# A one-core transformer layer on Trainium2: GpSimd paced by half slots, and expert outputs gathered in single transfers

## The chip, the core and the metric

The kernel runs on one core of one Trainium2 chip. The metric is the time of one execution on the device in microseconds (us); lower is better. The core's engines run side by side, each with its own instruction stream: TensorE (PE; its weight loads are shown as PEld), VectorE (DVE), ScalarE (ACT), GpSimd (POOL) and SyncE (SP), which only issues DMAs. They wait for each other through semaphores.

## What is computed

Token rows are gathered from an embedding table (4 batches of 512 tokens, 256 columns, 16 heads of 16). Two blocks follow, each behind a layer norm and added to its input:

```
h = take(W, ids)                                        # (4, 512, 256)
h = h + local_attention(layernorm(h)) @ Wo + bo         # window 128, looks one window back, causal
z = layernorm(h)
h = h + full_attention(z)                               # no mask
      + sum over the 2 best of 8 experts of gate * (z @ W_expert + b_expert)
```

## The kernel before

**Stages and slots.** The attention runs in eight stages, `STAGES`: local 0, local 1, local 2, full 0, local 3, full 1, full 2, full 3 (numbers 0 to 7; the number behind the kind is the batch). A stage has 16 slots (`u`), each of two half slots (`t`, 0 to 31). In every slot PE computes transposed scores into `ST` (L1414 in full stages, L1420 in local ones), row scores into `SC` (L1392) and probabilities times values into `OB` (L1441). ACT turns `ST` into `prob` (L800), DVE reduces `SC` to row maxima (L933). `SC` has two banks, so PE can be at most two row scores ahead of DVE.

**The other work** (projections, output projection, gates, expert matmuls, sums) hangs on the half slots by the table `PREPS`: an entry `(what, batch, first)` in stage s means that its steps are counted from half slot `first` of that stage; a negative `first` continues an entry of the stage before. All five engines walk through the same table in program order. A place in the table is a place in an engine's queue, not a time: an engine that waits for nothing runs ahead of the others.

**The experts.** Batches 0 and 1 (q = 0), then 2 and 3 (q = 1), go through the experts together. GpSimd scatters the normalised rows into `x_sorted` (8 indirect DMAs for each batch, 16 for each q; L611, `sort_rows`, from step 4 of `route` on). 24 tiles of sorted rows then run through the experts, two in every second half slot: GpSimd gathers each tile's weights (L625, `gather_weights`, into a ring of six), SP loads the rows (L517), PE turns and multiplies them (L1310, L1325), DVE copies the result to `ys` (L1088), and SP stores it to `y_sorted` (L524). At last `combine`: GpSimd gathers each token's two expert outputs from `y_sorted` (L645, `gather_outputs`; per batch four tiles of tokens, two transfers each) into six buffers `y` that lie in `xT_local`, `xT_full` and `rest`, and DVE adds them to `h` with their weights (L1102, `add_outputs`, five steps after the gather). GpSimd also adds the full attention to `h` (L682, `add_attention`), which waits for DVE's L975, and does the masks of the local stages (L672) and a part of the projections (L658).

**Where GpSimd can run ahead.** Its loop over the half slots has no wait of its own. In a local stage the mask of a slot waits for that slot's probabilities; in a full stage only waits inside the jobs hold it back, so transfers of several half slots can be issued behind each other.

## Time and profile before

| | |
|---|---|
| median of 3 runs | 676.07 us (670.94 to 677.17) |
| the profiled execution | 671.74 us, with a span of 670.0 us from the first to the last instruction |
| PE busy | 550.9 us, 82% of the span |
| DVE busy | 418.2 us, 62% |
| ACT busy | 304.0 us, 45% |
| GpSimd busy | 236.5 us, 35% |
| mean granted TensorE clock | 0.919 of full speed |

Busy time of an indirect DMA on GpSimd is the time in which it makes the transfer's descriptors, not the time in which the data moves. A wait is listed with what ended it; "remote" means that a semaphore ended it and that the profile found no instruction that ended just then. "issue" means that the profile shows no wait that ended just then.

### The profile page before, as it was taken

Reading aid. Unit: us, or ns where it says so; the run is one execution under the profiler, and the core shown is the slowest. Engines: PE = TensorE matmul, PEld = TensorE weight load, DVE = VectorE, ACT = ScalarE, POOL = GpSimd, SP = SyncE. Lnnn points to the kernel's source line nnn. Section 1 sums busy time; section 2 is a strip of 40 time slices with the busy share of each in tenths; the row PEclk is TensorE's granted clock in tenths of the full one; section 3 lists DMA queues with packets and bytes.
Section 4 is the critical chain, followed back from the end, with each engine's and each line's share of the span. In section 5 each row is a group of like instructions: output and inputs, shape, how many; then the busy total and the mean of one; then the engine's idle time right before and its main releaser. Section 6 shows DMA issues by size and latency. Waiting matters only on the chain.

```text
span 670.0 us, 9773 instructions
## 1 busy us (share of the span) xinstructions
PE 550.9 (82%) x3352; PEld 280.3 (42%) x3352; DVE 418.2 (62%) x927; ACT 304.0 (45%) x570; POOL 236.5 (35%) x294
## 2 busy tenths in 40 slices
PE   4765998989999899998869899889948648999562
PEld 3443554755654344444424455443312224554110
DVE  7336756667687876676688557558836427757620
ACT  0312545536445655662433554346625414545452
POOL 3853235224223300215462324121164264430721
PEclk9968899899999999996967999999978788999957
DMA  6387515433532255233253486733263566851320
GB/s 166 110 174 154 115 49 159 80 64 96 112 81 83 91 144 126 77 99 95 76 170 109 152 210 200 188 96 94 72 165 95 141 188 174 275 166 49 87 71 32
DMA packets 48049, 81.81 MB, mean 122 GB/s; under 512 B 7672, under 2 KB 39040, under 8 KB 44928
## 3 DMA queue, kind: packets, MB, share of 16 engines
q1 hardware_dynamic: 40320, 58.11, 33.5%
q0 software_dynamic: 7680, 23.08, 11.7%
q8 instruction: 27, 0.44, 0.3%
q14 instruction: 22, 0.18, 0.1%
HBM read 52.59 MB, written 28.31 MB: 121 GB/s over the span
## 4 chain that ended last, share of the span: by engine, by line
PE 60%; DVE 20%; issue 10%; another core or an unknown queue 3%; ACT 2%; DMA 2%; POOL 1%; SPq 0%; POOLq 0%; DVEq 0%; ACTq 0%
PE OB L1441 11%; PE SC L1392 8%; PE R L1234 8%; DVE neg_max L933 6%; PE ST L1414 6%; PE R L1325 5%; PE R L1249 5%; PE SC L1397 3%; PE ST L1420 2%; DMA QS<-shiftT 2%; PE R L1310 2%; PE R L1282 2%; PE R L1340 2%; PE SC L1400 2%
## 5 line engine op out<-in xcount | busy, mean ns | idle before, releaser
L933 DVE TENSOR_REDUCE neg_max<-SC 128x1 f32<-128x512 f32 x256 | 169.5, 686 | 120.7 <-PE SC L1392 86.0
L800 ACT ACTIVATE prob<-ST 128x512 f32<-128x512 f32 x256 | 136.8, 600 | 106.4 <-PE ST L1414 84.3
L1392 PE MATMUL SC<-KS,QS 96*128 96x512 bf16 x256 | 99.4, 400 | 44.1 <-DVE neg_max L933 29.7
L1441 PE MATMUL OB<-prob,VS 128*32 128x512 f32 (+2 forms) x1024 | 113.4, 517 | 0.1
L803 ACT ACTIVATE prob<-ST 128x512 f32<-128x512 f32 (+1 forms) x128 | 68.6, 543 | 82.0 <-PE ST L1420 76.3
L1414 PE MATMUL ST<-QS,KS 98*128 98x512 bf16 x256 | 82.1, 396 | 13.8 <-issue 12.3
L672 POOL TENSOR_SCALAR_AFFINE_SELECT prob<-prob 128x512 f32<-128x512 f32 x64 | 41.0, 640 | 138.7 <-ACT prob L803 135.5
L1392 PEld LDWEIGHTS SC<-KS,QS 96*128 96x128 bf16 x256 | 25.2, 98 | 97.6 <-DVE neg_max L933 66.8
L941 DVE TENSOR_REDUCE neg_max<-SC 128x2 f32<-128x512 f32 x64 | 44.1, 688 | 24.8 <-PE SC L1400 24.4
L1397 PE MATMUL SC<-KS,QS 96*128 96x256 bf16 (+1 forms) x256 | 55.8, 271 | 2.9 <-DVE neg_max L938 1.7
L938 DVE TENSOR_REDUCE neg_max<-SC 128x1 f32<-128x128 f32 (+1 forms) x128 | 39.5, 350 | 28.0 <-PE SC L1400 26.6
L1420 PE MATMUL ST<-QS,KS 98*128 98x256 bf16 (+1 forms) x256 | 49.5, 277 | 7.8 <-DMA QS<-shiftT 7.8
L1400 PE MATMUL SC<-mask_q,ident_bf 128*128 128x128 bf16 x256 | 52.0, 227 | 0.0
L658 POOL TENSOR_TENSOR parts<-rest,parts 128x512 bf16<-128x512 f32 x32 | 37.3, 1168 | 38.8 <-ACT parts L745 38.7
L682 POOL TENSOR_TENSOR h<-h,AO 128x256 f32<-128x256 f32 x16 | 11.6, 728 | 107.0 <-DVE AO L975 94.5
L1414 PEld LDWEIGHTS ST<-QS,KS 98*128 98x128 bf16 x256 | 24.7, 99 | 50.7 <-issue 23.2
L740 ACT ACTIVATE parts<-R,qk_bias 128x512 bf16<-128x512 f32 x32 | 22.0, 687 | 50.9 <-PE R L1234 49.8
L906 DVE SCALAR_TENSOR_TENSOR rest<-R,qk_bias,parts 128x512 f32<-128x512 f32 x32 | 23.9, 747 | 26.4 <-ACT parts L740 22.9
L1234 PE MATMUL R<-xT_full,w_qkv 128*128 128x512 f32 x64 | 33.8, 610 | 4.6 <-DVE VS L918 2.6
L1397 PEld LDWEIGHTS SC<-KS,QS 96*128 96x128 bf16 x256 | 25.5, 102 | 25.7 <-issue 9.5
L1441 PEld LDWEIGHTS OB<-prob,VS 128*32 128x32 f32 x1024 | 20.7, 111 | 34.6 <-issue 27.6
L1420 PEld LDWEIGHTS ST<-QS,KS 98*128 98x128 bf16 x256 | 23.2, 104 | 24.4 <-issue 16.7
(139 smaller groups left out, 816.1 us busy)
## 6 DMA issues: line engine op xcount, KB each, us to landing
scratch<-parts SPq DMA_DIRECT2D x96, 128.0 KB
QS<-scratch SPq DMA_DIRECT2D x16, 384.0 KB, 5.4
KS<-scratch SPq DMA_DIRECT2D x16, 384.0 KB, 4.7
xs<-x_sorted SPq DMA_DIRECT2D x24, 256.0 KB
y_sorted<-ys SPq DMA_DIRECT2D x24, 256.0 KB
QS<-scratch SPq DMA_DIRECT2D x16, 256.0 KB, 3.9
KS<-scratch SPq DMA_DIRECT2D x16, 256.0 KB, 4.9
x_sorted<-ys SPq DMA_DIRECT2D x24, 128.0 KB, 3.6
```

What stands on the lines that cost most here:

```text
L672: pool.affine_select(out=own, in_=own, compare_op=ALU.is_ge, fill=0.0, base=0, pattern=[[0, GH], [1, P]], channel_multiplier=-1).then_inc( ...
L800: act.activation(prob[:, u % 2, e, :], src[:, :], ACT.Exp, scale=SCALE).then_inc(s_prob, 1)
L803: act.activation(prob_local[:, u % 2, u // 2 % 2, 2 * e:2 * e + 2, 0:w], src[:, :].rearrange("p (i w) -> p i w", i=2)[:, :, 0:w], ACT.Exp, ...
L933: dve.tensor_reduce(own_max[:, i, head:head + 1], bank[:, :], AX.X, ALU.max, negate=True).then_inc(s_max, 1)
L941: dve.tensor_reduce(own_max[:, 2:4, head], bank[:, :].rearrange("p (w k) -> p w k", w=2), AX.X, ALU.max, negate=True).then_inc(s_max, 1)
L1234: mm = pe.matmul(bank[:, :], w, xT_of(p)[:, c, :], start=(c == 0), stop=(c == NC - 1))
L1392: pe.matmul(bank[:, :], Q[0:SHIFT_ROW, head, i * P:(i + 1) * P], K[0:SHIFT_ROW, head, :], start=True, stop=True).then_inc(s_sc_ps, 1)
L1397: pe.matmul(bank[:, first:last], Q[0:SHIFT_ROW, head, w * P:(w + 1) * P], K[0:SHIFT_ROW, head, max(w - 1, 0) * P:(w + 1) * P], start=(w % ...
L1400: mm = pe.matmul(bank[:, last - P:last], ident_bf[:, :], mask_q[:, :], start=False, stop=(w % 2 == 1), skip_group_check=True)
L1414: mm = pe.matmul(bank[:, :], K[0:KROWS, g * GH + e, keys], Q[0:KROWS, g * GH + e, :], start=True, stop=True)
L1420: mm = pe.matmul(bank[:, i * 2 * P:i * 2 * P + w], K[0:KROWS, head, keys], Q[0:KROWS, head, kt * P:kt * P + w], start=(i == 0), stop=(i == 1),
L1441: mm = pe.matmul(OB[VW * i:VW * (i + 1), columns], VS[s % 3][:, kt, v:v + VW], p_of, start=(kt == 0), stop=(kt == NT - 1), skip_group_chec ...
```

## The change

1. `PREPS`: `combine` of batch 0 moves from half slot 18 of stage 6 to half slot 30 of stage 5; `combine` of batch 1 from half slot 22 to half slot 21 of stage 6. Batches 2 and 3 stay.
2. `GATHERS`: for batches 0 and 1 one transfer is issued in a half slot instead of two (8 half slots instead of 4), and DVE's adds stand in every second half slot instead of every one. Batches 2 and 3 stay at two transfers.
3. From stage 4 on GpSimd waits at every half slot until PE has computed that half slot's first transposed scores (`begun`, a wait on `s_st_ps`). 128 waits are added; no other instruction is added or removed.

```diff
--- before.py
+++ after.py
@@ -64,9 +64,9 @@
     2: (("full", 0, -23), ("out", 1, 0), ("local", 3, 9)),
     3: (("out", 2, 0), ("full", 1, 9)),
     4: (("full", 1, -23), ("route", 0, 1), ("full", 2, 1), ("experts", 0, 33)),
-    5: (("experts", 0, 1), ("out", 3, 0), ("full", 3, 9)),
-    6: (("full", 3, -23), ("route", 1, 1), ("experts", 1, 19), ("combine", 0, 18), ("combine", 1, 22)),
-    7: (("experts", 1, -13), ("combine", 2, 16), ("combine", 3, 20)),
+    5: (("experts", 0, 1), ("out", 3, 0), ("full", 3, 9), ("combine", 0, 30)),
+    6: (("full", 3, -23), ("combine", 0, -2), ("route", 1, 1), ("experts", 1, 19), ("combine", 1, 21)),
+    7: (("experts", 1, -13), ("combine", 1, -11), ("combine", 2, 16), ("combine", 3, 20)),
 }
 START_SLOTS = 36
 HALF_SLOTS = 2 * UNITS
@@ -86,6 +86,7 @@
 ROUTE_STEPS = 13
 SCATTER_STEP = 4
 SCATTERS = (1, 2)
+GATHERS = (1, 1, 2, 2)
 W_RING, X_RING, Y_RING = 6, 3, 3
 LOAD_STEP, W_STEP, STORE_STEP, ADD_STEP = -4, -3, 6, 5
 
@@ -133,6 +134,12 @@
     after = STAGES[s + 1][0]
     first, end = (-(-TILES[after] * LEAD[after] * (head - H + j) // LEAD[kind]) for j in (0, 1))
     return [(s + 1, k) for k in range(first, end)]
+
+
+def begun(s, t):
+
+    per = BANKS[STAGES[s][0]]
+    return SCORES_BEFORE[s] + per * (t // 2) + per // 2 * (t % 2) + 1
 
 
 def first_rows(t):
@@ -628,24 +635,23 @@
                     bass.IndirectOffsetOnAxis(ap=w_rows[:, j:j + 1].bitcast(U32), axis=0),
                 ).then_inc(s_w_exp[n % W_RING], 16)
 
-            def gather_outputs(b, t):
+            def gather_output(b, t, k):
                 q, n = b // 2, b * NT + t
-                if n == 0:
+                if n == 0 and k == 0:
                     p = STAGE[FULL, B - 1]
                     pool.wait_ge(s_wo_ps, at(B - 1, 2, 2))
                     pool.wait_ge(s_v_ps, V_BEFORE[p + 1])
                     pool.wait_ge(s_qk_ps, at(p, 4, 4))
                     pool.wait_ge(s_part2, at(p, 4, 4))
-                if b % 2 == 0 and t == 0:
-                    for k in range(Y_RING):
-                        pool.wait_ge(s_stored[k], ring_count((q + 1) * TILE_JOBS - Y_RING + k, Y_RING))
-                if n >= len(y):
+                if b % 2 == 0 and t == 0 and k == 0:
+                    for j in range(Y_RING):
+                        pool.wait_ge(s_stored[j], ring_count((q + 1) * TILE_JOBS - Y_RING + j, Y_RING))
+                if n >= len(y) and k == 0:
                     pool.wait_ge(s_moe, 2 * (n - len(y) + 1))
-                for k in range(TOP_K):
-                    pool.indirect_dma_start(
-                        y[n % len(y)][:, k, :], None, y_sorted[q],
-                        bass.IndirectOffsetOnAxis(ap=slots[q][:, b % 2 * NT + t, k:k + 1].bitcast(U32), axis=0),
-                    ).then_inc(s_y[n % len(y)], 16)
+                pool.indirect_dma_start(
+                    y[n % len(y)][:, k, :], None, y_sorted[q],
+                    bass.IndirectOffsetOnAxis(ap=slots[q][:, b % 2 * NT + t, k:k + 1].bitcast(U32), axis=0),
+                ).then_inc(s_y[n % len(y)], 16)
 
             def inv_std(p):
                 pool.wait_ge(s_mv, at(p, 2, 2))
@@ -699,8 +705,10 @@
                     for j in range(EXPERT_TILES):
                         if step == W_STEP + j:
                             gather_weights(b, j)
-                if what == "combine" and 0 <= step < NT:
-                    gather_outputs(b, step)
+                if what == "combine":
+                    for n in range(NT * TOP_K):
+                        if step == n // GATHERS[b]:
+                            gather_output(b, n // TOP_K, n % TOP_K)
 
             for t in range(START_SLOTS):
                 if t == 2:
@@ -721,6 +729,8 @@
                     if kind == LOCAL:
                         mask(s, u)
                     for t in (2 * u, 2 * u + 1):
+                        if s >= STAGE[LOCAL, B - 1]:
+                            pool.wait_ge(s_st_ps, begun(s, t))
                         for what, c, first in PREPS[s]:
                             prep(what, c, t - first)
                     group = output_turned(s, u)
@@ -1131,8 +1141,10 @@
                         row_slots(b)
                     if step == 3:
                         tile_experts(b)
-                if what == "combine" and ADD_STEP <= step < ADD_STEP + NT:
-                    add_outputs(b, step - ADD_STEP)
+                if what == "combine":
+                    for t in range(NT):
+                        if step == ADD_STEP + t * TOP_K // GATHERS[b]:
+                            add_outputs(b, t)
 
             def half_slot(s, t, rows):
 
```

GpSimd's queue at the end of stage 5 and the start of stage 6, before, with what each instruction waits for (`x_sorted<-xn` are scatters for the experts, `w_` the gathers of expert weights, `y_sorted` as source the gathers of outputs, `h<-h,AO` the adds of the attention):

```order
L682 TENSOR_TENSOR h<-h,AO 128x4x64 [waits biases_added,group_normalised] x2
L611 DMA x_sorted<-xn_local,slots 3072x256 [waits sorted_rows_turned,route_steps,sorted_rows_zeroed]
L611 DMA x_sorted<-xn_local,slots 3072x256 x7
L611 DMA x_sorted<-xn_full,slots 3072x256 x6
L682 TENSOR_TENSOR h<-h,AO 128x4x64 [waits biases_added,group_normalised]
L611 DMA x_sorted<-xn_full,slots 3072x256 x2
L625 DMA w_q<-in_L_ffn_W_experts,w_rows 128x512 [waits experts_in_psum,route_steps]
```

And now. `transposed_scores` is the new wait for the half slot:

```order
L688 TENSOR_TENSOR h<-h,AO 128x4x64 [waits biases_added,group_normalised]
L651 DMA xT_local<-y_sorted,slots 128x256 [waits qk_in_psum,part2,v_in_psum,ys_stored0,projected,ys_stored1,transposed_scores,ys_stored2]
L651 DMA xT_local<-y_sorted,slots 128x256 [waits transposed_scores] x3
L651 DMA xT_full<-y_sorted,slots 128x256 [waits transposed_scores] x2
L688 TENSOR_TENSOR h<-h,AO 128x4x64 [waits biases_added,group_normalised]
L651 DMA xT_full<-y_sorted,slots 128x256 [waits transposed_scores] x2
L618 DMA x_sorted<-xn_local,slots 3072x256 [waits sorted_rows_turned,route_steps,sorted_rows_zeroed]
L618 DMA x_sorted<-xn_local,slots 3072x256
L618 DMA x_sorted<-xn_local,slots 3072x256 [waits transposed_scores]
L618 DMA x_sorted<-xn_local,slots 3072x256
```

Eight output gathers of batch 0 have come in ahead of the 16 scatters, six of them between two adds of the attention, and the scatters are held in pairs by the new wait.

GpSimd's queue from the first expert weights of q = 1 on, before:

```order
L625 DMA w_q<-in_L_ffn_W_experts,w_rows 128x512 [waits experts_in_psum,route_steps]
L625 DMA w_k<-in_L_ffn_W_experts,w_rows 128x512 [waits experts_in_psum]
L625 DMA w_v<-in_L_ffn_W_experts,w_rows 128x512 [waits experts_in_psum]
L645 DMA xT_local<-y_sorted,slots 128x256 [waits ys_stored0,part2,ys_stored1,qk_in_psum,ys_stored2,v_in_psum,projected]
L645 DMA xT_local<-y_sorted,slots 128x256
L625 DMA w_exp<-in_L_ffn_W_experts,w_rows 128x512 [waits experts_in_psum]
L645 DMA xT_local<-y_sorted,slots 128x256 x2
L682 TENSOR_TENSOR h<-h,AO 128x4x64 [waits biases_added,group_normalised]
L625 DMA w_exp<-in_L_ffn_W_experts,w_rows 128x512 [waits experts_in_psum]
```

And now:

```order
L688 TENSOR_TENSOR h<-h,AO 128x4x64 [waits biases_added,group_normalised]
L632 DMA w_exp<-in_L_ffn_W_experts,w_rows 128x512 [waits experts_in_psum,transposed_scores] x2
L651 DMA rest<-y_sorted,slots 128x256
L632 DMA w_q<-in_L_ffn_W_experts,w_rows 128x512 [waits experts_in_psum,transposed_scores]
L651 DMA rest<-y_sorted,slots 128x256
L632 DMA w_k<-in_L_ffn_W_experts,w_rows 128x512 [waits experts_in_psum,transposed_scores]
L651 DMA rest<-y_sorted,slots 128x256
L632 DMA w_v<-in_L_ffn_W_experts,w_rows 128x512 [waits experts_in_psum,transposed_scores]
L651 DMA rest<-y_sorted,slots 128x256
L632 DMA w_exp<-in_L_ffn_W_experts,w_rows 128x512 [waits experts_in_psum,transposed_scores]
L651 DMA xT_local<-y_sorted,slots 128x256 [waits expert_output_added]
```

Where one weight gather and two output gathers of batches 0 and 1 stood for a half slot, there are now one weight gather and one output gather of batch 1, each half slot behind a wait.

DVE's queue in half slots 2 to 5 of stage 6, before:

```order
L1078 TENSOR_TENSOR h<-R,h 128x512
L933 TENSOR_REDUCE neg_max<-SC 128x1
L950 CAST shift<-neg_max 128x4x4
L952 TENSOR_TENSOR shift<-neg_max,shift 128x4x4
L1055 TENSOR_TENSOR picked<-pick,position 128x128
L1058 TENSOR_REDUCE slot_f<-picked 128x16
L1059 CAST slots<-slot_f 128x16
L933 TENSOR_REDUCE neg_max<-SC 128x1
```

And now, in the same place:

```order
L1088 TENSOR_TENSOR h<-R,h 128x512
L943 TENSOR_REDUCE neg_max<-SC 128x1
L960 CAST shift<-neg_max 128x4x4
L962 TENSOR_TENSOR shift<-neg_max,shift 128x4x4
L1112 SCALAR_TENSOR_TENSOR h<-xT_local,weight,h 128x256 x2
L1065 TENSOR_TENSOR picked<-pick,position 128x128
L1068 TENSOR_REDUCE slot_f<-picked 128x16
L1069 CAST slots<-slot_f 128x16
L943 TENSOR_REDUCE neg_max<-SC 128x1
```

The first two adds of batch 0 (one pair of instructions for each tile of tokens) stand in half slot 3, ahead of the last steps that give the scatters their row numbers; the other three pairs follow in half slots 5, 7 and 9.

## Rows read from the trace of the kernel before

**Rows 1.** Waits of DVE: in total, times, longest, in us

```profile
DVE neg_max L933 <- remote: 25.6, 4, 11.4
```

**Rows 2.** Timeline 480 to 504: start, duration, instruction, [idle before <- ended by]

```profile
483.49 1.15 POOL L611 DMA_INDIRECT x_sorted<-xn_local,slots  x1 [0.15 <-issue]
...
495.30 0.39 PE L1392 MATMUL SC<-KS,QS 96*128 96x512 bf16 x1 [1.17 <-issue]
...
500.08 0.96 POOL L611 DMA_INDIRECT x_sorted<-xn_full,slots  x1 [0.30 <-issue]
...
502.33 0.69 DVE L933 TENSOR_REDUCE neg_max<-SC 128x1 f32<-128x512 f32 x1 [7.09 <-remote]
...
503.08 0.61 PE L1392 MATMUL SC<-KS,QS 96*128 96x512 bf16 x1 [7.40 <-issue]
```

**Rows 3.** Timeline 505 to 545, the second run of transfers

```profile
511.13 0.98 POOL L611 DMA_INDIRECT x_sorted<-xn_full,slots  x1 [0.16 <-issue]
...
522.48 0.95 POOL L645 DMA_INDIRECT xT_local<-y_sorted,slots  x1 [0.30 <-issue]
...
526.35 0.61 PE L1392 MATMUL SC<-KS,QS 96*128 96x512 bf16 x1 [5.25 <-DVE neg_max L933]
```

**Rows 4.** Timeline 534 to 554, the third run

```profile
535.05 0.96 POOL L625 DMA_INDIRECT w_exp<-in_L_ffn_W_experts,w_rows  x1 [0.15 <-issue]
...
543.49 0.38 PE L1392 MATMUL SC<-KS,QS 96*128 96x512 bf16 x1
...
548.82 0.95 POOL L645 DMA_INDIRECT rest<-y_sorted,slots  x1 [0.30 <-issue]
...
553.09 0.61 PE L1392 MATMUL SC<-KS,QS 96*128 96x512 bf16 x1 [9.22 <-DVE neg_max L933]
```

**Rows 5.** Timeline 620 to 641, the fourth run, in stage 7

```profile
620.97 0.94 POOL L645 DMA_INDIRECT xT_full<-y_sorted,slots  x1 [22.37 <-DMA y_sorted<-ys]
...
628.83 0.82 PE L1414 MATMUL ST<-QS,KS 98*128 98x512 bf16 x3
...
632.50 0.95 POOL L645 DMA_INDIRECT xT_local<-y_sorted,slots  x1 [0.30 <-issue]
...
635.29 1.00 DVE L1102 SCALAR_TENSOR_TENSOR h<-xT_local,weight,h 128x256 f32<-128x256 f32 x2 [1.41 <-DMA xT_local<-y_sorted,slots]
...
640.00 0.61 PE L1414 MATMUL ST<-QS,KS 98*128 98x512 bf16 x1 [10.35 <-issue]
```

**Rows 6.** Timeline 366 to 377, the six first weight gathers

```profile
367.24 0.99 POOL L625 DMA_INDIRECT w_q<-in_L_ffn_W_experts,w_rows  x1 [0.46 <-issue]
...
373.55 0.95 POOL L625 DMA_INDIRECT w_exp<-in_L_ffn_W_experts,w_rows  x1 [0.30 <-issue]
...
375.81 1.29 DVE L933 TENSOR_REDUCE neg_max<-SC 128x1 f32<-128x512 f32 x2 [2.13 <-remote]
```

**Rows 7.** PE alone, 505 to 545: half slots 12, 17, 22, 24 of stage 6 begin

```profile
507.63 0.60 PE L1414 MATMUL ST<-QS,KS 98*128 98x512 bf16 x2
...
516.62 0.60 PE L1414 MATMUL ST<-QS,KS 98*128 98x512 bf16 x2
...
537.61 0.60 PE L1414 MATMUL ST<-QS,KS 98*128 98x512 bf16 x2
...
543.05 0.60 PE L1414 MATMUL ST<-QS,KS 98*128 98x512 bf16 x2
```

**Rows 8.** Busy time by window: us, PE, PEld, DVE, ACT, POOL busy, clock, DMA share, GB/s

```profile
468.00:483.50 15.50, 14.96 (x92) 5.56 (x92) 14.05 (x35) 9.73 (x18) 0.74 (x2) 1.00 0.21 69
503.00:511.00 8.00, 7.59 (x36) 2.06 (x36) 5.07 (x12) 4.34 (x8) 0.72 (x1) 0.75 0.12 34
```

**Rows 9.** SP's DMA issues: last stores of expert outputs, q = 0 and q = 1

```profile
473.09 0.46 SPq L524 DMA_DIRECT2D y_sorted<-ys  x1
...
617.31 0.95 SPq L524 DMA_DIRECT2D y_sorted<-ys  x2
```

**Rows 10.** DVE's timeline, 479 to 485: the row numbers of the scatters

```profile
480.36 0.28 DVE L1055 TENSOR_TENSOR picked<-pick,position 128x128 f32<-128x128 f32 x1
```

## The prediction, made before the changed kernel ran

> **What bounds the kernel now.** I read the waits first. DVE's row maxima wait four times, 25.6 us in all, for a semaphore whose update matches no instruction that ended just then [rows 1]. The timelines around these waits show the same picture each time. From 483.49 to 500.08 GpSimd starts 14 scatters, one each 1.28 us. PE's row score of 495.30 ends at 495.69; the reduction that needs only this score starts at 502.33, 6.6 us late, and PE's next matmul at 503.08, after 7.4 us of idle time [rows 2]. DVE, ACT and PE have nothing else to wait for. So what is late is the news of PE's finished work, and it comes 1.3 us after GpSimd's run ends (501.04 to 502.33). The second run lasts from 511.13 to 523.43, and PE idles 5.25 us up to 526.35 [rows 3]. The third, 12 transfers from 535.05 to 549.77, ends in 9.2 us of idle PE up to 553.09 [rows 4]. The fourth begins at 620.97 in stage 7: PE ends its scores at 629.65 and starts again at 640.00, 10.35 us later [rows 5]. Six weight gathers from 367.24 to 374.50 leave DVE idle for 2.13 us up to 375.81 [rows 6]. Five runs, five pauses: 34 us of 671.74, of which PE idles 32. A pause sets in 5 to 10 us after a run began. After a pause the matmuls run at the lower clock level, 1.2 GHz (0.61 us for one that took 0.39 before, [rows 2]); in the 8 us after the first pause the granted clock is 0.75 [rows 8], at most 2.0 us lost. I take 1.2 us for each of the first three.
>
> DVE's four waits of [rows 1] all lie in these runs. That GpSimd's unbroken run of transfers is the cause is a reading of five coincidences, not a measured fact. I build the sum on it, and the second rival on its failure. Elsewhere in stages 5 to 7 PE is busy nearly all the time, so work on GpSimd costs only through these pauses and through what it delivers late.
>
> **The change, part by part.** The waits themselves are cheap. In stage 4 each slot's mask already waits for that slot's probabilities, which PE's scores precede: nothing changes. In stage 5 the first six weight gathers are no longer one run: the third must wait for half slot 0 of stage 5, the next ones for 1, 2 and 3. That takes away the pause of [rows 6]: **-1.7 us** (0 if it stays). Later weight gathers wait for experts two half slots or less before their own half slot anyway; a delay up to one half slot is covered by the four to five half slots between gather and use.
>
> *Batch 0's gathers.* They are now first in line at half slot 30 of stage 5, but they need the last store of q = 0, which SP issues at 473.09, ending 473.55 [rows 9]. In stage 7 the last store's issue ended at 618.26 and the gather started at 620.97, 2.7 us later [rows 5, 9]; so the first starts at about 476.3, when PE has already reached half slot 2 of stage 6. The waits hold none of the first six: one each 1.26 us, until 483.8. The attention's add (0.7 us) and two more gathers follow, to 487.2. Then come the scatters, which began at 483.49 before. Behind the waiting gather on GpSimd only the add and these scatters are queued; SP's row loads need the scatters, but not before half slot 15.
>
> *DVE's adds.* A gather that starts at 632.50 has its add at 635.29, 2.8 us later [rows 5]. So the first tile of tokens is there at 476.3 + 1.3 + 2.8 = 480.4, and DVE comes to that place at 480.36 [rows 10]: a wait of 0 to 0.6 us. Each pair of adds takes 1.0 us [rows 5]. In this stretch DVE is busy 14.05 of 15.5 us [rows 8], so the pair of half slot 3 is paid in full, and of the three others in half slots 5, 7 and 9 I count half. Where they stood, beside the experts, PE's slots are longer (5.4 us for two half slots, [rows 7], against 3.6) with expert matmuls that DVE doesn't set, and I count nothing back. **+3.0 us** (0 to 4.6).
>
> The Trainium skill (DMA: Bandwidth & Descriptors, Anatomy of one DMA) fits a GpSimd transfer with 2.0 us plus bytes over 436 GB/s, 2.3 us for these 128 KB. By it the tile is there at 479.9 and the wait is surely nil; by the row it is 480.4, and the sum is the same within 0.6 us.
>
> *The first pause.* The run now begins at 476.3 instead of 483.49. Let the pause set in at 484, PE being in half slot 5 or 6. Here the new wait acts: with PE's news late, GpSimd sees no further half slot begin and may issue only what is released, the last gathers and the pair of scatters of half slot 5, until 489.7. The pause ends 1.3 to 2.5 us later, near 491.5: 7.5 us, as long as the 7.4 of before. **0.** The other scatters are two to a half slot, 2.5 us of issue in half slots that take 1.8 us each (507.63 to 516.62 for five, [rows 7]), so GpSimd falls behind again and runs without a gap for 8 to 12 transfers: I add **+2 us** for a second, short pause (0 to 8).
>
> *The second pause.* The 10 transfers of [rows 3] were 2 scatters, 4 weight gathers and 4 output gathers. The output gathers are gone, and the weights come one to a half slot, 1.26 us of issue in 1.8. I take the pause away: 5.25 + 1.2 = **-6.5 us** (-6.5 to -3).
>
> *The third pause.* The 12 transfers of [rows 4] were three for each half slot. Now there are two, from half slot 21 to 28, 5.0 us of issue in a slot of 5.4 (537.61 to 543.05, [rows 7]). The gaps are 0.4 us, where 0.3 us lies between transfers anyway, so I don't expect it to vanish. But again GpSimd can issue only what has begun, at most four transfers. I take two pauses of 2 to 2.5 us for one of 9.2 with its 1.2 of slow clock: **-6 us** (-12 to 0).
>
> *The fourth pause* stays: batches 2 and 3 keep two transfers a half slot, and the gathers start only when the last store has landed, at 620.97 [rows 5], when half slots 16 and 17 of stage 7 have already begun. **0** (-6 to +2).
>
> Sum: -1.7 + 3.0 + 0 + 2 - 6.5 - 6 = -9.2 us, against the profiled execution's 671.74: 662.5. The median of the three runs, 676.07, stands 4.3 us above this execution; I allow 1.5 us for that and say **664 us**, 1.8% below the median.
>
> **The rivals.** *First, all of stage 6's pauses go.* A wait at each half slot could already be gap enough; then the first pause's 7.4 + 1.2, the second's 6.5 and the third's 10.4 go, with 1.7 of stage 5, and 3 for the adds stays: 671.7 - 24.2 = 647.5. For it: no pause stands in stage 4, where pairs of scatters alternate with masks. Against it: the runs of stage 6 keep next to no gap by the arithmetic above.
>
> *Second, the pauses move and don't shrink,* because their cause is not the unbroken issue but, say, the number of transfers in flight, or other DMA traffic: 671.7 + 3 for the adds, less some luck, 668 to 677, no measurable change. For it: the pauses set in after 5 us in one run and 10 in another, which a plain count of transfers doesn't give. Against it: all five coincide with runs, and none lies elsewhere.
>
> The Trainium skill (SBUF — State Buffer, Who interferes with whom) speaks for this rival: its rule is that "PE and ACT never wait on anyone", and GpSimd's interference is with VectorE alone. By that rule spacing the transfers frees nothing on PE, and the time is the second rival's; by rows 2 to 6 PE's idle time follows GpSimd's runs. No run yet separates the two.
>
> *Third, slower.* 8 gathers and 14 scatters stand in one line from 476.3 on, 28 us of issue with only one add of 0.7 us between. If the new waits hold GpSimd less than I think, because PE's scores of the next half slots are told before the freeze, the pause lasts from 484 to 505.5 instead of 7.4 us: +14; with the third pause unchanged the sum is 671.7 - 1.7 + 3 + 14 - 6.5 = 680.5. It decides from about 12 us of first pause on. Against it: in [rows 2] PE starts one more score after 494 and then nothing, so half slots that have begun can't pile up during a pause.
>
> **How the numbers follow.** Chances: my forecast 0.40, the first rival 0.18, the second 0.28, the third 0.14. The forecast's own range is 654 to 672, from the bounds of the second, third and adds' terms. The whole range, to hold 8 in 10, reaches to both outer cases: 646 to 680. A measurement of this kernel can tell about 1% from no change. Faster by over 1% (below 669.3) holds nearly all of the forecast and the first rival, 0.56; within 1%, the second and the forecast's upper end, 0.31; slower, the third, 0.13.
>
> **What would show it.** In the new profile: the first output gather near 476 to 477, the scatters from about 487; no idle time of PE over 3 us between half slots 14 and 19 of stage 6; shorter ones between 21 and 28; one of about 10 us near the end of stage 7; and DVE's waits for a "remote" semaphore down from 25.6 us to under 15. The prediction is wrong if pauses of the old length stand beside short runs of transfers, or if GpSimd's waits for its half slots show up as late weights at the expert matmuls.

## The result and the profile after

The changed kernel takes 650.26 us (median of 4 runs, 646.69 to 653.42) against 673.51 us (4 runs, 669.59 to 677.17) of the kernel before: a ratio of 0.9641, 95% interval 0.9599 to 0.9683, 3.6% faster. The forecast was 664 us, 1.8% faster: the direction and the range hold, the gain is twice as large. On other chips it is different, and that is the larger surprise; the experiments come to it.

The profiled execution took 652.53 us, its span is 650.8 us against 670.0 us before, at a mean granted clock of 0.933 against 0.919. The lines of after bear other numbers: L943 is L933 of before, L1404 is L1392, L1426 is L1414, L1453 is L1441, L1112 is L1102, L651 is L645, L618 is L611, L632 is L625, L810 is L800.

The three largest waits of the kernel after for a semaphore whose update matches no instruction that ended just then (in total, times, longest, in us):

```profile
ACT prob L810 <- remote: 9.9, 4, 4.5
DVE neg_max L943 <- remote: 7.4, 3, 3.6
ACT shiftT L790 <- remote: 7.3, 1, 7.3
```

DVE's 25.6 us of [rows 1] have become 7.4. To see where the time went, I cut stages 6 and 7 at the same half slots in both kernels, by the starts of PE's first transposed scores of half slots 0, 12, 19 and 30 of stage 6 and 22 of stage 7. The windows of before (in each: length, PE busy and instructions, the other engines, granted clock, DMA):

```profile
core 0: us, PE busy (x) PEld busy (x) DVE busy (x) ACT busy (x) POOL busy (x), PEclk, DMA share, GB/s
471.30:507.60 36.30, 25.26 (x126) 7.64 (x125) 21.07 (x44) 15.33 (x28) 14.33 (x15) 0.81 0.41 114
507.60:526.70 19.10, 10.95 (x57) 2.95 (x56) 9.83 (x18) 8.34 (x16) 10.28 (x11) 0.93 0.60 163
526.70:573.20 46.50, 35.19 (x173) 17.55 (x172) 24.73 (x49) 17.30 (x32) 22.29 (x24) 0.85 0.54 147
573.20:628.80 55.60, 53.60 (x293) 25.24 (x291) 37.75 (x70) 31.50 (x59) 16.34 (x18) 1.00 0.48 156
628.80:670.00 41.20, 17.03 (x78) 3.70 (x76) 8.38 (x19) 12.17 (x23) 12.23 (x14) 0.68 0.20 61
```

and the same of after:

```profile
471.60:510.00 38.40, 28.93 (x127) 8.16 (x126) 25.14 (x52) 15.33 (x28) 22.24 (x23) 0.78 0.49 132
510.00:521.20 11.20, 10.47 (x58) 2.95 (x57) 9.52 (x18) 8.40 (x16) 5.07 (x6) 1.00 0.32 105
521.20:556.80 35.60, 32.59 (x174) 17.19 (x173) 20.93 (x40) 17.22 (x32) 19.17 (x22) 0.95 0.82 219
556.80:613.00 56.20, 53.54 (x293) 25.21 (x291) 38.01 (x70) 30.73 (x58) 17.24 (x19) 1.00 0.48 156
613.00:650.80 37.80, 15.59 (x78) 3.62 (x76) 8.28 (x19) 12.92 (x25) 12.25 (x14) 0.75 0.22 66
```

PE issues the same matmuls. The second window loses 7.9 us: PE's idle time falls from 8.15 to 0.73. The third loses 10.9: 8.3 us of idle time, and 2.6 of busy time because the clock is granted at 0.95 instead of 0.85. The last loses 3.4, the first gains 2.1, the fourth 0.6.

The first window of after in the timeline (start, duration, instruction, [idle before <- ended by]):

```profile
478.52 0.96 POOL L651 DMA_INDIRECT xT_local<-y_sorted,slots  x1 [11.12 <-DMA y_sorted<-ys]
...
482.69 1.01 DVE L1112 SCALAR_TENSOR_TENSOR h<-xT_local,weight,h 128x256 f32<-128x256 f32 x2 [1.75 <-DMA xT_local<-y_sorted,slots]
...
485.30 0.61 PE L1404 MATMUL SC<-KS,QS 96*128 96x512 bf16 x1 [3.25 <-issue]
...
489.48 1.01 POOL L618 DMA_INDIRECT x_sorted<-xn_local,slots  x1 [0.30 <-issue]
...
493.82 0.61 PE L1404 MATMUL SC<-KS,QS 96*128 96x512 bf16 x1
...
497.23 0.69 DVE L943 TENSOR_REDUCE neg_max<-SC 128x1 f32<-128x512 f32 x1 [3.59 <-remote]
497.51 0.97 POOL L618 DMA_INDIRECT x_sorted<-xn_local,slots  x1 [0.53 <-remote]
...
497.98 0.39 PE L1404 MATMUL SC<-KS,QS 96*128 96x512 bf16 x1 [2.31 <-issue]
...
501.26 0.97 POOL L618 DMA_INDIRECT x_sorted<-xn_full,slots  x1 [1.51 <-remote]
```

The first output gather starts 2.2 us later than forecast, the scatters at 489.48. The pause of [rows 2], 7.40 us in one piece, is gone. What is late now are the maxima of 497.23: DVE waits 3.59 us for them, 2.8 of these after PE's score of 493.82 had ended (494.43), and PE idles 2.31 us up to 497.98; GpSimd's own waits for its half slots (497.51 and 501.26) stand beside it. The 3.25 us up to 485.30 are not of this kind: the adds of batch 0 stand ahead of the maxima in DVE's queue, and the first pair waits 1.75 us for its tile (482.69). In the window PE's idle time falls from 11.0 to 9.5 us, and its busy time grows by 3.7, at a clock of 0.78. The end of stage 7:

```profile
605.00 0.94 POOL L651 DMA_INDIRECT xT_full<-y_sorted,slots  x1 [21.89 <-PE ST L1426]
...
619.20 0.94 POOL L651 DMA_INDIRECT xT_local<-y_sorted,slots  x1 [0.30 <-issue]
622.28 0.57 ACT L790 COPY shiftT<-R 8x512 bf16<-8x512 bf16 x1 [7.32 <-remote]
622.55 0.94 POOL L651 DMA_INDIRECT xT_full<-y_sorted,slots  x1 [2.41 <-remote]
623.39 0.61 PE L1426 MATMUL ST<-QS,KS 98*128 98x512 bf16 x1 [7.99 <-ACT prob L810]
```

Here GpSimd issues 12 transfers in a row from 605.00, then has to wait for half slot 22. PE's news reaches ACT at 622.28, 2.1 us after GpSimd fell still (619.20 + 0.94), and PE's idle time is 7.99 us instead of the 10.35 of [rows 5].

### The profile page after: what moved, and what is told of

The parts are those of the page before. It is cut to its first block, busy times and chain, and to the rows that moved or that the text cites. A ratio compares the mean times of both kernels' runs of the same rounds, so it can differ in the third digit from the quotient of the medians.

```text
span 650.8 us, 9845 instructions
## 1 busy us (share of the span) xinstructions
PE 547.8 (84%) x3352; PEld 279.3 (43%) x3352; DVE 416.7 (64%) x927; ACT 304.0 (47%) x570; POOL 237.5 (36%) x294
## 3 DMA queue, kind: packets, MB, share of 16 engines
q0 software_dynamic: 7680, 23.08, 11.7%
## 4 chain that ended last, share of the span: by engine, by line
PE 63%; DVE 20%; issue 7%; DMA 2%; POOL 2%; ACT 2%; another core or an unknown queue 2%; SPq 0%; POOLq 0%; DVEq 0%; ACTq 0%
PE OB L1453 12%; PE SC L1404 8%; PE R L1246 8%; PE R L1337 7%; DVE neg_max L943 6%; PE ST L1426 6%; PE R L1261 5%; PE SC L1409 3%; PE R L1322 3%; PE ST L1432 3%; DMA QS<-shiftT 2%; PE R L1294 2%; PE R L1352 2%; PE SC L1412 2%
## 5 line engine op out<-in xcount | busy, mean ns | idle before, releaser
L943 DVE TENSOR_REDUCE neg_max<-SC 128x1 f32<-128x512 f32 x256 | 169.0, 685 | 102.4 <-PE SC L1404 85.5
L810 ACT ACTIVATE prob<-ST 128x512 f32<-128x512 f32 x256 | 137.1, 600 | 101.5 <-PE ST L1426 80.7
L1404 PE MATMUL SC<-KS,QS 96*128 96x512 bf16 x256 | 98.8, 398 | 29.8 <-DVE neg_max L943 16.7
L1453 PE MATMUL OB<-prob,VS 128*32 128x512 f32 (+2 forms) x1024 | 113.5, 517 | 0.1
L1426 PE MATMUL ST<-QS,KS 98*128 98x512 bf16 x256 | 80.9, 391 | 11.3 <-ACT prob L810 9.1
L1404 PEld LDWEIGHTS SC<-KS,QS 96*128 96x128 bf16 x256 | 25.1, 98 | 84.7 <-DVE neg_max L943 51.8
L951 DVE TENSOR_REDUCE neg_max<-SC 128x2 f32<-128x512 f32 x64 | 44.0, 688 | 25.6 <-PE SC L1412 25.3
L664 POOL TENSOR_TENSOR parts<-rest,parts 128x512 bf16<-128x512 f32 x32 | 37.7, 1181 | 37.4 <-ACT parts L755 26.5
L750 ACT ACTIVATE parts<-R,qk_bias 128x512 bf16<-128x512 f32 x32 | 22.0, 687 | 50.3 <-PE R L1246 48.7
L1426 PEld LDWEIGHTS ST<-QS,KS 98*128 98x128 bf16 x256 | 24.8, 99 | 47.0 <-ACT prob L810 22.3
L1409 PEld LDWEIGHTS SC<-KS,QS 96*128 96x128 bf16 x256 | 25.6, 102 | 26.5 <-issue 9.3
L688 POOL TENSOR_TENSOR h<-h,AO 128x256 f32<-128x256 f32 x16 | 11.6, 727 | 64.8 <-DVE AO L985 56.4
L1453 PEld LDWEIGHTS OB<-prob,VS 128*32 128x32 f32 x1024 | 20.7, 111 | 33.2 <-issue 28.2
```

The source lines that it names most:

```text
L810: act.activation(prob[:, u % 2, e, :], src[:, :], ACT.Exp, scale=SCALE).then_inc(s_prob, 1)
L943: dve.tensor_reduce(own_max[:, i, head:head + 1], bank[:, :], AX.X, ALU.max, negate=True).then_inc(s_max, 1)
L951: dve.tensor_reduce(own_max[:, 2:4, head], bank[:, :].rearrange("p (w k) -> p w k", w=2), AX.X, ALU.max, negate=True).then_inc(s_max, 1)
L1404: pe.matmul(bank[:, :], Q[0:SHIFT_ROW, head, i * P:(i + 1) * P], K[0:SHIFT_ROW, head, :], start=True, stop=True).then_inc(s_sc_ps, 1)
L1409: pe.matmul(bank[:, first:last], Q[0:SHIFT_ROW, head, w * P:(w + 1) * P], K[0:SHIFT_ROW, head, max(w - 1, 0) * P:(w + 1) * P], start=(w % ...
L1426: mm = pe.matmul(bank[:, :], K[0:KROWS, g * GH + e, keys], Q[0:KROWS, g * GH + e, :], start=True, stop=True)
```

## The experiments

**Theory A**: while GpSimd issues indirect transfers without a break, the semaphore updates of PE (news of finished matmuls) reach the other engines late, after 5 to 10 us of such a run, and are let through when GpSimd pauses. The new waits are a feedback: once PE's news is late, GpSimd runs out of released work and stops. **Theory B**: the pauses come from the number of transfers or the traffic, and waits alone change nothing; the gain is that of the moved gathers.

*The parts of the change.* `waits_only` and `waits_2` are one kernel: the kernel before with the waits alone.

```diff
                     for t in (2 * u, 2 * u + 1):
+                        if s >= STAGE[LOCAL, B - 1]:
+                            pool.wait_ge(s_st_ps, begun(s, t))
                         for what, c, first in PREPS[s]:
```

> The kernel before with the third part of the change alone: from stage 4 on GpSimd waits for every half slot; the table and the gathers stay two to a half slot. Theory A (PE's news is late once GpSimd has issued indirect DMAs without a break for 5 to 10 us, and a wait that stops GpSimd ends the lateness): the waits cut the runs of 14, 10, 12 and 16 transfers as soon as PE stands still, so the pauses of 7.4, 5.3, 9.2 and 10.4 us shrink by a third to a half each; time 655 to 663. Theory B (the pauses come from the number or the traffic of the transfers, the gain of the change from moving the gathers out of the expert part): no pause shrinks by more than 1 us; 668 to 675.

> The waits alone, again. Theory A: on a chip with pauses in the kernel before, they cut the runs of transfers and shorten the pauses of 7.4, 5.3, 9.2 and 10.4 us by a third to a half: ratio 0.975 to 0.99. On a chip without pauses 1.00. Theory B (the gain comes from the moved gathers): 1.00 on both.

`moves_only` and `moves_2` are the changed kernel without these two lines.

> The changed kernel without its waits: the gathers of batches 0 and 1 moved and one to a half slot in the table, but nothing holds GpSimd. Theory A: 8 gathers and 14 scatters follow each other with one add of 0.7 us between, from about 478 on; PE pauses from about 486 to 507, some 15 to 20 us instead of 7.4; the second pause is gone (-6.5), the third is a run of 12 to 16 and stays near 9; 670 to 682. Theory B: the waits do nothing, and the time is that of the changed kernel, 647 to 654.

> The moved gathers without the waits, again. Theory A: on a chip with pauses, the unbroken run of 22 transfers from 478 on makes one of 15 to 20 us; ratio 0.99 to 1.02. On a chip without, 1.009 as before. Theory B: 0.965 on a chip with pauses.

`after_2` and `after_3` are the changed kernel itself.

> The changed kernel again, beside the kernel before. On the chip of the four runs so far PE's news was never late and the kernel before took 624.9 us; on the chip of the prediction's runs it took 673.5. Theory A (lateness of PE's news during GpSimd's runs is a property of some chips, and the change gains only there): where the kernel before takes 670 or more, the change gives 0.96 to 0.97; where it takes about 625, it gives 1.00 to 1.01, since the moved adds cost and no pause is there to save. Theory B (the change gains by its order of work too): under 0.99 on either chip.

> The changed kernel again, as the partner of the two kernels with breaks. On a chip with pauses (kernel before about 674 us) 648 to 653 us, ratio 0.96 to 0.972. On a chip without (about 625 us) only the moved adds and gathers show: ratio 1.000 to 1.010, 625 to 631 us; if the new waits of GpSimd cost something by themselves it would be above 1.010.

Two kinds of chip came up in these runs. On chips 9 and 7 the kernel before takes 625 us (19 runs each), on chips 3, 2 and 1 it takes 674:

| kernel | chip 3 (before 673.99) | chip 9 or 7 (before 624.86, 625.00) |
|---|---|---|
| waits alone | 658.70, 0.9772 (0.9699 to 0.9844) | 625.13, 1.0006 (0.9981 to 1.0030) |
| moves alone | 664.36, 0.9855 (0.9791 to 0.9920) | 630.59, 1.0090 (1.0064 to 1.0115) |
| both | 650.99, 0.9679 (0.9596 to 0.9762) | 630.78, 1.0090 (1.0062 to 1.0119) |

On chip 3 the first two rows rest on two runs each and the third on three. The chip of the result, which is not named, behaves as chip 3. On chips 9 and 7 the change makes the kernel 0.9% slower, all of it by the moves, and the waits cost nothing. There is no pause there: in none of the traces from them does any engine wait for a "remote" semaphore, though GpSimd issues as densely (the kernel before itself has no trace from such a chip; its nearest are `run12` and the waits alone). The last run of the changed kernel on chip 7 (start, duration, instruction, [idle before <- ended by]):

```profile
593.61 0.95 POOL L651 DMA_INDIRECT xT_full<-y_sorted,slots  x1 [21.88 <-PE ST L1426]
...
604.22 0.82 PE L1426 MATMUL ST<-QS,KS 98*128 98x512 bf16 x3 [0.54 <-DMA QS<-shiftT]
...
605.36 0.39 PE L1426 MATMUL ST<-QS,KS 98*128 98x512 bf16 x1 [0.32 <-ACT prob L810]
...
612.68 0.95 POOL L651 DMA_INDIRECT xT_full<-y_sorted,slots  x1 [0.30 <-issue]
```

Sixteen transfers stand without a gap from 593.61 to 613.63, and PE waits 0.3 to 0.5 us between its scores, not 8 to 10.

On chip 3 both parts gain (2.3% and 1.5%), and together 3.2%, which the intervals don't tell from the sum. Neither theory says all of that. Theory B falls with `waits_2`, and its 0.965 for `moves_2` is missed as well. A is borne out by the ratio of `waits_2`, though not pause by pause, and missed by `moves_2`: I had expected 0.99 to 1.02 and a pause of 15 to 20 us. In lengths between half slots, in us (worked out from the traces as above; the kernel before on the result's chip, `late_moves` and `mid_moves` of further below on chips 2 and 1, waits alone on chip 9 as the one without pauses):

| | stage 6, 0 to 12 | 12 to 19 | 19 to 24 | 24 to stage 7 | stage 7, 0 to 22 | 22 to 31 | 31 to end |
|---|---|---|---|---|---|---|---|
| before | 36.3 | 19.1 | 16.4 | 35.6 | 50.1 | 25.5 | 15.7 |
| waits_2 | 31.2 | 14.4 | 21.1 | 33.7 | 50.3 | 21.3 | 15.7 |
| moves_2 | 44.6 | 14.7 | 15.4 | 26.5 | 50.3 | 26.6 | 15.7 |
| after_2 | 38.9 | 11.2 | 14.9 | 27.3 | 50.4 | 22.0 | 15.7 |
| late_moves | 32.8 | 11.4 | 18.4 | 27.6 | 58.1 | 21.7 | 15.7 |
| mid_moves | 32.3 | 17.9 | 17.4 | 27.5 | 50.3 | 22.2 | 15.7 |
| waits_only, chip 9 | 26.1 | 11.7 | 14.9 | 24.5 | 49.8 | 11.6 | 16.1 |
| after_3, chip 7 | 29.7 | 11.1 | 18.9 | 22.8 | 49.8 | 11.5 | 16.4 |

The waits alone shorten the first pause (half slots 0 to 12, by 5.1 us) and the one at the end of stage 7 (by 4.2). The second they only move on: half slots 12 to 24 take 35.5 us with them and without, and the third shrinks by 1.9. The moves alone thin out what lies behind half slot 12, at the price of 8.3 us ahead of it, where 8 gathers and 14 scatters now stand in one run with one add between. Two late waits beside that run in `moves_2`, of DVE and ACT, one of its later scatters, and ACT's wait at the end of stage 7:

```profile
496.44 0.69 DVE L941 TENSOR_REDUCE neg_max<-SC 128x1 f32<-128x512 f32 x1 [5.68 <-remote]
497.92 0.60 ACT L808 ACTIVATE prob<-ST 128x512 f32<-128x512 f32 x1 [8.69 <-remote]
...
502.49 0.97 POOL L618 DMA_INDIRECT x_sorted<-xn_full,slots  x1 [0.30 <-issue]
...
633.86 0.57 ACT L788 COPY shiftT<-R 8x512 bf16<-8x512 bf16 x1 [12.93 <-remote]
```

The last row is the end of stage 7 without the new waits: ACT waits 12.9 us behind the unbroken 16 transfers, against 7.32 us in the changed kernel. The first two show something that Theory A hadn't said: PE's news came through at 496.44 and 497.92 although GpSimd went on issuing until 503.46. In the kernel before the fourth pause ends in the same way:

```profile
637.91 0.57 ACT L780 COPY shiftT<-R 8x512 bf16<-8x512 bf16 x1 [9.18 <-remote]
...
640.01 0.95 POOL L645 DMA_INDIRECT xT_full<-y_sorted,slots  x1 [0.30 <-issue]
```

So the end of a run isn't what every pause waits for; late news also arrives in the middle of a run, and what lets it through then stays open. That explains why `moves_2` has two pauses of PE (5.73 us up to 497.19 and 3.85 up to 503.03) and not one of 15 to 20.

The price of the moves without pauses is read from chips 9 and 7: `after_3` against `waits_only` is 3.6 us longer in half slots 0 to 12 and 4.0 in 19 to 24, and 1.7 shorter behind. How it is shared out is less sure than the sum: `moves_only` against `run12` (30.8, 11.2, 17.0 and 22.8 us in stage 6 against 26.0, 11.2, 16.0 and 24.0) makes it 4.8, 1.0 and −1.2, with 4.6 us in all against 5.3. At the first of these places in `moves_only`:

```profile
480.36 1.00 DVE L1110 SCALAR_TENSOR_TENSOR h<-xT_local,weight,h 128x256 f32<-128x256 f32 x2 [1.28 <-DMA xT_local<-y_sorted,slots]
...
483.01 0.61 PE L1402 MATMUL SC<-KS,QS 96*128 96x512 bf16 x1 [2.62 <-DVE neg_max L941]
```

DVE waits 1.28 us for the first tile of tokens, adds it in 1.00, and PE idles 2.62 us for the maxima queued behind.

*A pause made on purpose.* `run12` and `run12_2` are the kernel before with 12 extra gathers of 128 KB in one run in stage 3, where no pause was; they land in buffers that are free then, and nothing uses what they bring.

```diff
+            def extra_run():
+                pool.wait_ge(s_st_ps, begun(3, 16))
+                for k in range(12):
+                    dst = (w_exp[3 + k // 2] if k < 6 else xs[(k - 6) // 2])[:, k % 2, :]
+                    pool.indirect_dma_start(dst, None, tok_w,
+                        bass.IndirectOffsetOnAxis(ap=ids[:, k:k + 1].bitcast(U32), axis=0),
+                    ).then_inc(s_extra, 16)
```

Left out of this cut and of the next two are the new semaphore and the waits of GpSimd and SP for all 12 landings, which stand ahead of the first expert weights and the first expert rows.

> The kernel before with 12 more indirect gathers of 128 rows of the embedding table (128 KB each) into buffers that are free then, issued by GpSimd behind each other at half slot 16 of stage 3, where no pause stood. Nothing uses what they fetch; GpSimd and SP wait for them only in stage 4. Theory A: 12 transfers take 15 us of issue; PE's news is late from 6 to 10 us after the first on and comes 1 to 2.5 us after the last: a new pause of 6 to 10 us in stage 3, span 676 to 681. Theory B (other traffic or places make the pauses): no idle time of PE over 3 us there, span within 2 us of 670.

> Twelve additional gathers in one run in stage 3, again. Theory A: on a chip with pauses a new one of 6 to 10 us in stage 3, PE idle from about 265 to 273; on a chip without, none. Theory B (the pauses need something else of stages 6 and 7): none in stage 3 on either.

`run12_gap4`, `run12_gap4_2` and `run12_gap4_3` have the same 12 with two breaks:

```diff
+                    if k in (3, 7):
+                        pool.wait_ge(s_extra, 16 * (k + 1))
```

> The same 12 additional gathers at the same place, but after the 4th and the 8th GpSimd waits until they have landed (about 1.8 us). Theory A: runs of four are too short for a pause, or a break of 1.8 us ends the lateness: idle time of PE there under 2 us, span 670 to 673. Theory B: what counts is the number or the bytes, so this does what the run of 12 does, whatever that is.

> The kernel before with the same 12 extra row gathers in the first full stage as in the run of 12, but now GpSimd waits after the 4th and the 8th until all issued so far have landed, a break of 1.5 to 2 us each time. Theory A (TensorE's news is held back while GpSimd issues indirect transfers without a break, and is let through once it pauses for 1.2 us or more): no new pause or one under 2 us at 259 to 280 us, time 671 to 675 against 673 to 674 of the kernel before on such a chip. Rival (the number of transfers counts, by the bytes or descriptors they put into the queues): a pause of 5 us or more as in the unbroken run, 678 to 682. On a chip where the kernel before takes about 625 us neither shows.

> The same kernel as the one with 12 extra gathers and breaks after the 4th and 8th, whose first two runs fell on a chip that has no pauses. Theory A (TensorE's news is held back while GpSimd issues indirect transfers without a break, let through once it pauses): on a chip with pauses no new pause or one under 2 us at 259 to 280 us, time 671 to 675 where the kernel before takes 673 to 674. Rival (the number of transfers counts): a pause of 5 us or more, 678 to 682. Where the kernel before takes about 625 us neither shows.

`run12_sp` issues 12 plain transfers of the same size into the same buffers from SP's queue instead:

```diff
+                        for k in range(12):
+                            dst = (w_exp[3 + k // 2] if k < 6 else xs[(k - 6) // 2])[:, k % 2, :]
+                            sp.dma_start(dst, tok_w[k * P:(k + 1) * P, :]).then_inc(s_extra, 16)
```

> The kernel before, with 12 plain transfers of 128 KB each issued by the SP queue in the place where the run of 12 GpSimd gathers stood (first full stage), into the same buffers. Theory A (GpSimd's issuing of indirect transfers is what holds TensorE's news back): no new pause at 258 to 275 us, the half slots 19 to 21 of that stage about 4 us apart, 672 to 675 where the kernel before takes 674. Rival (any 1.5 MB of traffic does): half slots 7 us apart as with the 12 gathers, 678 to 682. On a chip without pauses it tells nothing.

On chips 9 and 7 none of them shows anything (623.98, 626.26, and 625.43 us at 1.0002, 0.9971 to 1.0033). On the others:

| kernel | chip | half slots 19, 20, 21 of stage 3 start at | time, ratio |
|---|---|---|---|
| before | of the result | 266.6, 270.0, 274.0 | |
| 12 in one run (`run12_2`) | 3 | 267.5, 275.2, 282.0 | 680.77 (one run; before 673.99) |
| 4 + 4 + 4 (`run12_gap4_3`) | 2 | 266.0, 269.4, 273.4 | 675.35, 1.0001 (0.9960 to 1.0041) |
| 12 plain ones from SP (`run12_sp`) | 1 | 267.2, 270.5, 274.5 | 675.28, 1.0015 (0.9993 to 1.0037) |

The unbroken run, `run12_2`:

```profile
258.76 1.08 POOL L719 DMA_INDIRECT w_exp<-in_L_tok_W,ids  x1 [5.67 <-PE ST L1435]
...
267.98 0.38 PE L1413 MATMUL SC<-KS,QS 96*128 96x512 bf16 x1
...
272.45 0.69 DVE L954 TENSOR_REDUCE neg_max<-SC 128x1 f32<-128x512 f32 x1 [3.88 <-remote]
272.66 0.94 POOL L719 DMA_INDIRECT xs<-in_L_tok_W,ids  x1 [0.30 <-issue]
273.85 1.12 PE L1361 MATMUL R<-ident,OT 128*128 128x128 f32 x4 [3.41 <-DVE rest L927]
```

and with breaks, `run12_gap4_3`:

```profile
266.62 0.95 POOL L719 DMA_INDIRECT w_exp<-in_L_tok_W,ids  x1 [4.54 <-DMA w_exp<-in_L_tok_W,ids]
266.86 0.69 DVE L956 TENSOR_REDUCE neg_max<-SC 128x1 f32<-128x512 f32 x1 [0.42 <-PE SC L1415]
...
273.58 0.95 POOL L719 DMA_INDIRECT xs<-in_L_tok_W,ids  x1 [2.26 <-DMA xs<-in_L_tok_W,ids]
```

In the first the score of 267.98 ends at 268.36 and its reduction starts at 272.45; the news that is late is 9.6 us younger than the first transfer. From the start of half slot 19 to that of 21 it takes 14.5 us where it took 7.4. Up to the start of half slot 22, a stretch with the same matmuls, it is 17.7 us against 9.7, at a granted clock of 0.71 against 1.00: 3.7 us more of idle time and 4.3 more of busy time, so the slow clock costs more than the standing still. In the second the same reduction waits 0.42 us.

So 12 transfers in one run make a pause, 12 in three runs don't, and the same 1.5 MB from SP's queue doesn't. The number of the transfers isn't the cause; the unbroken issuing on GpSimd is, and this half of Theory A stands for this kind of chip. The other half, that the news is let through when GpSimd pauses, fails here too: the reduction of 272.45 starts before the 12th transfer (272.66). Three things limit the result. The unbroken run is a single execution. The three kernels ran on three chips, so a difference between those chips isn't excluded. And SP issues its 12 in 5.8 us, GpSimd in 14.8: that traffic kept up as long as GpSimd's, or plain transfers from GpSimd, would do nothing is not tested.

*Where the gathers stand.* `late_moves` keeps the waits and one output gather a half slot, but begins at half slot 18 of stage 6 as before (batch 1 behind batch 0), with the stores of the results to match (left out of the cut):

```diff
-    5: (("experts", 0, 1), ("out", 3, 0), ("full", 3, 9), ("combine", 0, 30)),
-    6: (("full", 3, -23), ("combine", 0, -2), ("route", 1, 1), ("experts", 1, 19), ("combine", 1, 21)),
-    7: (("experts", 1, -13), ("combine", 1, -11), ("combine", 2, 16), ("combine", 3, 20)),
+    5: (("experts", 0, 1), ("out", 3, 0), ("full", 3, 9)),
+    6: (("full", 3, -23), ("route", 1, 1), ("experts", 1, 19), ("combine", 0, 18), ("combine", 1, 26)),
+    7: (("experts", 1, -13), ("combine", 1, -6), ("combine", 2, 16), ("combine", 3, 20)),
```

> The changed kernel with batch 0's and batch 1's output gathers still one transfer a half slot and with the new waits, but begun where they stood before (half slot 18 of the second-last stage), batch 1's behind them to half slot 33; the adds and the stores of these batches later to match. Theory A (the feedback and the spreading bring the gain, the earlier place costs the adds on VectorE 0.9% on a chip without pauses): 0.96 to 0.97 of the kernel before where it takes about 674 us, and 0.997 to 1.003 where it takes about 625 us. Rival C (the earlier place is what brings the moves' gain, since it thins the half slots 16 to 32 of the second-last stage): 0.975 to 0.985, as the waits alone, on a chip with pauses; and on one without them 1.005 or more, since the late adds stand where TensorE runs at its upper clock.

657.28 us on chip 2, 0.9764 (0.9693 to 0.9836): in all no more than the waits alone. But stage 6 is 10.2 us shorter than with these (90.2 us for 100.4, in the table above), and even 2.1 shorter than in `after_2`. What that gains is lost behind: the first 22 half slots of stage 7 take 58.1 us instead of 50.3, because output gathers now stand up to its half slot 1, beside the weight gathers, and a pause falls there:

```profile
562.77 0.69 DVE L943 TENSOR_REDUCE neg_max<-SC 128x1 f32<-128x512 f32 x1 [5.56 <-remote]
```

`mid_moves` puts batch 0 at half slot 13, behind the scatters, and leaves batch 1 at 21.

> The changed kernel, with batch 0's output gathers begun at half slot 13 of the second-last stage, behind the first half slots' scatters (5 to 12) instead of ahead of them, one a half slot to 20; batch 1's stay at 21. The adds follow (half slots 18, 20, 22, 24). Theory A (the 8 gathers from 478 us and the 8 first scatters behind them are one unbroken run, and its adds block VectorE at half slots 3 to 9): where the kernel before takes about 674 us the pauses at 490 to 502 us become shorter, and 0.955 to 0.968; where it takes about 625 us the changed kernel's loss of 0.9% goes, 0.998 to 1.004. Rival D (half slots 13 to 20 then hold 16 weight gathers and output gathers, a new unbroken run, as where the gathers stood in their old place): 0.970 to 0.980 on a chip with pauses, and 1.000 to 1.006 on one without.

656.23 us on chip 1, 0.9724 (0.9694 to 0.9754). The stretch of half slots 0 to 12 takes 32.3 us instead of the 38.9 of the changed kernel, and 12 to 24 takes 35.3 instead of 26.1. The scatters end, and the gathers go on in their stead:

```profile
515.51 1.30 ACT L810 ACTIVATE prob<-ST 128x512 f32<-128x512 f32 x2 [2.97 <-remote]
515.75 0.95 POOL L632 DMA_INDIRECT w_k<-in_L_ffn_W_experts,w_rows  x1 [1.25 <-remote]
...
541.07 0.59 ACT L783 COPY xsT<-R 128x512 f32<-128x512 f32 x1 [3.78 <-remote]
541.94 0.95 POOL L632 DMA_INDIRECT w_v<-in_L_ffn_W_experts,w_rows  x1 [2.73 <-remote]
```

So the early place is what the moves' gain comes from: it keeps the stretch of the expert weights free of output gathers. Spreading them in the late place thins that stretch as well, but only pushes the pause into stage 7. The three kernels ran on different chips. The intervals of `late_moves` and `mid_moves` lie just clear of the changed kernel's first one (0.9599 to 0.9683), and meet that of `after_2` (0.9596 to 0.9762).

*Breaks for the changed kernel.* `after_gap4` lets GpSimd wait for the landing after every 4th scatter and every 4th output gather of batches 2 and 3, `after_gap2` after every 2nd, `last_gap` and `last_gap_2`, which are one kernel, only after every 4th of the last 16 gathers (this is their edit; the other two have the like behind the scatters too):

```diff
                 ).then_inc(s_y[n % len(y)], 16)
+                if b >= 2 and (t * TOP_K + k + 1) % 4 == 0:
+                    pool.wait_ge(s_y[n % len(y)], 2 * ring_count(n, len(y)))
```

> The changed kernel, with GpSimd waiting for the landing after every 4th scatter of the rows and after every 4th output gather of batches 2 and 3 (about 1.8 us each, 12 breaks). Theory A: what is left of the pauses, at the first scatters (3 to 4 us of idle TensorE), at the second ones (about 3) and at 620 us (8), goes to a large part: 10 us or more below the changed kernel, 636 to 643 us where that takes 650, pauses of TensorE each under 2.5 us. Rival B (GpSimd's breaks make its own work late: the scatters end 6 us later and the expert loads with them): no gain or a loss, 650 to 656. On a chip without pauses: within 0.3% of the changed kernel by A, 0.5% or more slower by B.

> As the one with a break after every 4th transfer, but after every 2nd (24 breaks, 43 us of waiting in all). Theory A with a limit between 2 and 4 transfers in a row: 3 us or more below the version with breaks after 4. If 4 in a row are already harmless: equal to it within 2 us, or slower by what the longer scatter run makes late (the second pair's scatters then take about 40 us instead of 20 and the expert loads behind them start late): up to 5 us slower.

These two ran on chip 7: 647.11 us, 1.0328 (1.0277 to 1.0379), and 672.02 us, 1.0751 (1.0706 to 1.0795), where the changed kernel has 1.009. Theory A's "within 0.3%" for `after_gap4` on such a chip is missed, and the rival holds: where there is no pause to remove, breaks only make GpSimd late. In `after_gap4` the scatters of q = 1 end late, and PE waits for their rows:

```profile
527.34 1.10 PE L1327 MATMUL R<-ident,xs 128*128 128x128 f32 x4 [7.18 <-DMA xs<-x_sorted]
```

15.57 us stand in that place with breaks after every 2nd. Neither was run on a chip with pauses.

> The changed kernel, with GpSimd waiting for the landing after every 4th of the last 16 output gathers (batches 2 and 3), nothing else. Theory A: on a chip with pauses the one at 612 to 620 us (8 us of idle TensorE) shrinks to under 3 us, but each break makes the last adds later (2 to 5 us from the end by the run with breaks everywhere): together 645 to 650 us, ratio 0.957 to 0.966. Rival (what is left at 620 us has another cause): the pause stays and the breaks cost 4 to 6 us, 654 to 657, ratio 0.971 to 0.977. On a chip without pauses: 4 to 6 us slower than the changed kernel, 1.015 to 1.019.

> The same kernel as last_gap (the changed one with breaks after every 4th of the last 16 output gathers), in more rounds. Theory A: on a chip with pauses 0.955 to 0.962 of the kernel before, below the changed kernel's 0.964 and 0.968. If its first result was luck: 0.963 to 0.970. On a chip without pauses the breaks only make the last adds later: 1.015 to 1.019 against the changed kernel's 1.009; above 1.009 by 0.005 at least.

On chip 1 `last_gap` takes 646.98 us, 0.9585 (0.9522 to 0.9648), the lowest ratio of this study, though its interval meets those of the changed kernel. Half slots 22 to 31 of stage 7 take 12.6 us instead of 22.0, the length of a chip without pauses; half slot 31 to the end takes 20.1 instead of 15.7, because the last adds wait for the last gathers:

```profile
611.34 0.94 POOL L651 DMA_INDIRECT rest<-y_sorted,slots  x1 [2.07 <-DMA xT_full<-y_sorted,slots]
...
625.05 1.14 POOL L651 DMA_INDIRECT xT_full<-y_sorted,slots  x1 [2.03 <-DMA xT_local<-y_sorted,slots]
...
629.28 1.00 DVE L1114 SCALAR_TENSOR_TENSOR h<-xT_full,weight,h 128x256 f32<-128x256 f32 x2 [3.40 <-DMA xT_full<-y_sorted,slots]
```

A gain of 9.4 us for a loss of 4.4. On chip 10 (before 626.61) only the losses remain, that of the moves and that of the breaks: 638.00 us, 1.0172 (1.0119 to 1.0225), with 21.5 us from half slot 31 to the end against the 16.4 of `after_3`. The remaining pause at the end was of the same cause. No version here is best on both kinds of chip: the waits alone cost nothing on the one and gain 2.3% on the other.

## Why the prediction was right and where it was wrong

The gain was forecast at 9.2 us and measured at 19.2. The cause was right; the step that failed is the sizing of the pauses, of the third one first (−6 for −10.9), then of the fourth (0 for −3.4), the stretch of the first (+5 for +2.1) and the second (−6.5 for −7.9). A later start of stage 4 (2.0) and 0.6 us in stage 7 go the other way.

*What bounds the kernel*: right on these chips. "What is late is the news of PE's finished work" holds, and GpSimd's unbroken runs are the cause (`run12_2` against `run12_gap4_3` and `run12_sp`, with the limits said there). Not right is that the news waits for the end of the run: that fits four of the five pauses of [rows 2 to 6], but the fourth is over while GpSimd still issues (637.91 and 640.01 above). The first pause also sets in later than the "5 to 10 us" of the prediction: PE's idle time begins at 495.69, 12.2 us after the first transfer. The second rival falls for these chips. The Trainium skill's rule that spoke for it (SBUF — State Buffer, Who interferes with whom: "PE and ACT never wait on anyone") doesn't help it: in `run12_2` PE idles 3.41 us up to 273.85 beside a GpSimd that only issues transfers, by way of late news, while the page speaks of the memory's ports. On chips 9, 7 and 10 PE has no such wait.

*The pause of stage 5*, −1.7 us: of that size between the two profiles (stage 4 begins 2.0 us later in after, stage 6 only 0.3 later), but not shown as I argued it. Four weight gathers still go in one run, and DVE's wait of 2.13 us [rows 6] has a like one in after:

```profile
371.92 0.95 POOL L632 DMA_INDIRECT w_exp<-in_L_ffn_W_experts,w_rows  x1 [0.30 <-issue]
374.19 0.94 POOL L632 DMA_INDIRECT w_exp<-in_L_ffn_W_experts,w_rows  x1 [1.33 <-PE ST L1426]
```

```profile
373.93 1.29 DVE L943 TENSOR_REDUCE neg_max<-SC 128x1 f32<-128x512 f32 x2 [2.07 <-PE SC L1404]
```

Stage 5 takes 102.2 to 102.6 us in every kernel with the waits on such chips (`waits_2`, `after_2`, `late_moves`, `mid_moves`, `last_gap`) and 103.2 to 103.3 in before, `moves_2` and `run12_2`, but 105.4 and 105.5 in `run12_gap4_3` and `run12_sp`, which lack the waits as well. By these traces the waits take at least 0.6 us off stage 5; how much more, and by which wait, is open.

*The adds*, +3.0 us: near for their first place (3.6 to 4.8 us on chips without pauses), but I counted nothing where gathers and adds of batch 1 stand; there half slots 19 to 24 grow by 1.0 to 4.0 us and the rest of the stage shrinks by 1.2 to 1.7. The moves cost 4.6 to 5.3 us in all without pauses, not 3.0. The first gather was placed too early: I took 2.7 us from the end of SP's last store, as in stage 7, and it took 4.7 (473.85 to 478.52), so DVE's wait was 1.75 us and not 0 to 0.6. On a chip with pauses the second part doesn't show (14.4 to 14.9 us in half slots 19 to 24 for 16.4 before).

*The first pause and the second, short one*, 0 and +2, with the adds +5: measured +2.1. Without pauses the moves cost 3.6 to 4.8 us here, so the pauses' part is −1.5 to −2.7, not +2. The feedback did what I had said of it (GpSimd stops ahead of 497.51 and 501.26), and the runs it leaves make no second idle time of PE of 2 us (the longest is 1.47, up to 505.39).

*The second pause*, −6.5 us: measured −7.9 in half slots 12 to 19. I had the idle time (−7.4) as 5.25 alone; the rest are three shorter waits of PE for DVE's maxima (1.09, 0.61 and 0.72 us up to 516.40, 517.83 and 520.70 in the trace of before). The clock gave back 0.5 where I had counted 1.2.

*The third pause* is the term that was sized worst, and the step that failed first of all: −6 us forecast, −10.9 measured in half slots 19 to 30. I put two pauses of 2 to 2.5 us in the place of the one; there is one of 2.44, at which GpSimd stops as well (2.84 us up to 538.94), and 3.0 us of idle time of PE in all. The slow clock, which I had taken at 1.2 us, gave back 2.6. The sentence that failed is "The gaps are 0.4 us, where 0.3 us lies between transfers anyway, so I don't expect it to vanish." `moves_2` shows that the thinner half slots alone do it (26.5 us from half slot 24 on, for 35.6), without the feedback; the waits alone leave 33.7.

*The fourth pause*, 0 forecast, −3.4 measured. This is the second step that failed. I took it that the waits would not act there since half slots 16 and 17 had begun. But only 12 of the 16 gathers were released (those of half slots 16 to 21), the last 4 were not, and GpSimd stopped at 620.14 instead of running through; ACT's late wait fell from 12.93 us (`moves_2`) to 7.32. That is the feedback I had used for the first pause and forgotten here.

The measured steps from stage 4 on are 2.0 of a later start, −1.7, +2.1, −7.9, −10.9 and −3.4, with 0.6 for the fourth window: −19.2 us, the difference of the spans. The forecast was −9.2 against its own execution. Its range of 654 to 672 doesn't quite come from its terms: with their upper ends the sum is +1.9 us, and 673.6 before anything is added for the median. The clock was priced too low as well: waits_only on chip 9 does the matmuls of stages 6 and 7 in 132.2 us of busy time, the kernel before in 142.0, so the pauses of before cost 9.8 us by the clock beside 34 of idle time, where I had counted 1.2 for each of three.

*What no step of the prediction had*: that the pauses belong to some chips only. On the other kind the true answer is 0.9% slower, and nothing in the profile of before could say how common that is. Six chips were named in these runs: 3, 2 and 1 with pauses, 9, 7 and 10 without. What differs in them stays open; the landings that GpSimd waits for are not slower (a break in the last run lasts 2.03 to 2.07 us on chip 1, 2.04 to 2.09 on chip 10).

## What to carry to other kernels

Where engines stand still together and each waits for news of work that has long ended, look for a queue that issues transfers without a break, and give it a reason to stop: a wait on the progress of the engine whose news is late costs nothing where there is no such pause (1.0006, 0.9981 to 1.0030), and where there are some it shortened the first and the last here, though it only moved the second on. Price a pause with the slow clock behind it, and price moved work at both of its ends. Measure on more than one chip before a gain that rests on such a pause is called the kernel's.

## What was not expected of the hardware

The same kernel takes 674 us on some chips and 625 us on others, 7% less, with the same instructions and transfers. On the first kind ACT waits up to 12.9 us for PE's news behind 16 indirect transfers of GpSimd one after another, on the second nothing is late behind the same 16 (593.61 to 613.63 us on chip 7). The news of DVE, ACT and GpSimd is in time meanwhile: of the updates that the traces of before and after hold, only those of PE's finished matmuls come more than a microsecond behind their end. Plain transfers that SP issues don't do it: 12 in 5.8 us (258.76 to 264.56) moved nothing.

The traces themselves differ between the two kinds of chip, too. Those of chips 9, 7 and 10 hold 6261 to 6468 marks of landed transfers and lack at most 3 semaphore updates of each of PE, DVE and ACT. Those of the result's chip and of chips 3, 2 and 1 hold 4552 to 4885 such marks, and lack 45 to 80 updates of each of the three engines. So records get lost there that the other kind keeps. Every time in this document comes from an execution for which a span and a clock were recorded. Whether the recording takes part in the pauses is a rival that no run here tests.
